# Reordered row loads, weight loads and row normalisation in a two-layer gated cross-attention kernel

## The reference

```python
x = x + tanh(g_xattn[0]) * _L0_xattn_ref(_layernorm(x), ctx_512, Wq, w_kc_q, w_kc_kv, W_qr, W_kr, Wo)
x = x + tanh(g_ffn[0])   * _L0_ffn_ref(_layernorm(x), Wr, br, W1, b1, W2, b2, A1, B1, A2, B2)
x = x + tanh(g_xattn[1]) * _L1_xattn_ref(_layernorm(x), ctx_512, Wq, Wkv_expand, Wout)
x = x + tanh(g_ffn[1])   * _L1_ffn_ref(_layernorm(x), U, V, W1, b1, W2, b2)
...
# _L0_xattn_ref: 16 heads
q_r = einsum('bshq,hqr->bhsr', einsum('bshk,hkq->bshq', q_hk, w_kc_q), W_qr)
scores = einsum('bhsr,bhlr->bhsl', q_r, einsum('bld,hdr->bhlr', kv_rope, W_kr))
attn = softmax(scores)                       # called P in the kernel
ctx_c = einsum('bhsl,bld->bhsd', attn, kv_rope)
out = einsum('bhsd,hkd->bshk', ctx_c, w_kc_kv).reshape(b, s, H * K) @ Wo.T
...
# _L1_ffn_ref: 8 low-rank experts, mixed softly
alpha = softmax(relu(x @ W1 + b1) @ W2 + b2)
vx = einsum('krd,bsd->bskr', V, x)
out = einsum('bsk,bskd->bsd', alpha, einsum('kdr,bskr->bskd', U, vx))
```

## Time and profile before

| | us |
|---|---|
| three runs, median | 1366.28 (1364.13 to 1367.78) |
| profiled execution, its own time | 1366.01 |
| its span | 1364.2 |
| TensorE busy in the span | 1338.5 (98%) |
| VectorE / ScalarE / GpSimd busy | 937.1 / 519.0 / 408.3 |
| DMA, mean over the span | 108 GB/s |

### The profile page before, as it was taken

How to read it: one execution, slowest core, us unless ns; L and a number is a source line. 1 busy time by engine, 2 the same in 40 slices (tenths; PEclk the granted TensorE clock), 3 DMA queues, 4 the chain that set the end, 5 groups by cost and what they waited for, 6 DMA issues and landing times.

```text
span 1364.2 us, 20490 instructions
## 1 busy us (share of the span) xinstructions
PE 1338.5 (98%) x7532; PEld 1083.8 (79%) x7532; DVE 937.1 (69%) x1803; ACT 519.0 (38%) x1569; POOL 408.3 (30%) x463
## 2 busy tenths in 40 slices
PE   7999999999999999999999999999999999999999
PEld 5788888888878788778887888788876788878777
DVE  5666676675775878785778667866888777746533
ACT  2545445455554321231123111311137777712220
POOL 3113313232255343101111111114418865530000
PEclk9999999999999999999999999999999999999999
DMA  8655444443563232210221012112333131144431
GB/s 273 211 164 172 153 157 149 151 157 125 179 208 97 80 94 71 81 39 16 67 89 43 20 43 90 31 58 66 116 110 121 46 103 63 56 142 147 136 124 54
DMA packets 120136, 146.73 MB, mean 108 GB/s; under 512 B 14157, under 2 KB 75725, under 8 KB 120037
## 3 DMA queue, kind: packets, MB, share of 16 engines
q1 hardware_dynamic: 120036, 145.44, 33.5%
HBM read 101.35 MB, written 44.04 MB: 107 GB/s over the span
## 4 chain that ended last, share of the span: by engine, by line
PE 84%; DVE 9%; DMA 2%; SPq 1%; issue 1%; POOL 1%; ACT 1%; DVEq 0%; ACTq 0%; POOLq 0%
PE bank L118 80%; PE bank L121 3%; SPq L170 1%; DVE AH L130 1%; DVE STG L130 1%; DVE st L152 1%; DVE XR L140 1%; DVE PYZ L164 1%; DMA XR<-scr 1%; DVE sm L143 1%; DMA PYZ<-pscr 1%; DVE PT L130 0%; DVE XR L137 0%; DVE AH L127 0%; ACT STG L124 0%
## 5 line engine op out<-in xcount | busy, mean ns | idle before, releaser
L118 PE MATMUL bank<-XT,AR 128*128 128x512 f32 x1152 | 280.2, 393 | 0.1
L118 PE MATMUL bank<-AR 128*128 128x512 f32 x1056 | 260.5, 396 | 1.1 <-DVE PTV L127 0.7
L118 PEld LDWEIGHTS bank<-XT,AR 128*128 128x128 f32 x1152 | 213.9, 188 | 48.5 <-issue 1.5
L124 ACT ACTIVATE STG<-bank,b1c 128x512 f32<-128x512 f32 x128 | 88.3, 690 | 387.2 <-PE bank L118 319.2
L118 PEld LDWEIGHTS bank<-AR 128*128 128x128 f32 x1056 | 193.7, 188 | 46.1 <-DVE AR L130 1.5
L118 PE MATMUL bank<-AR,CT 128*128 128x512 f32 x768 | 191.3, 392 | 0.0
L118 PE MATMUL bank<-AR,AH 128*128 128x512 f32 x768 | 185.8, 390 | 0.0
L127 DVE CAST AH<-STG 128x512 fp32r<-128x512 f32 x192 | 91.3, 475 | 112.8 <-PE bank L118 98.8
L118 PEld LDWEIGHTS bank<-AR,AH 128*128 128x128 f32 x768 | 143.6, 188 | 30.7 <-issue 1.1
L118 PEld LDWEIGHTS bank<-AR,CT 128*128 128x128 f32 x768 | 140.1, 188 | 27.0 <-issue 0.4
L127 POOL CAST BA<-STG 128x256 fp32r<-128x256 f32 x64 | 31.2, 488 | 395.9 <-PE bank L118 251.8
(11 more groups left out here) (142 smaller groups left out, 1858.1 us busy)
## 6 DMA issues: line engine op xcount, KB each, us to landing
XR<-scr SPq DMA_DIRECT2D x64, 256.0 KB, 2.9
pscr<-PYZ SPq DMA_DIRECT2D x30, 512.0 KB, 2.7
PYZ<-pscr SPq DMA_DIRECT2D x120, 128.0 KB, 3.0
XR<-in_x_dram SPq DMA_DIRECT2D x32, 256.0 KB, 4.1
XR<-lscr SPq DMA_DIRECT2D x128, 64.0 KB, 2.0
scr<-XR SPq DMA_DIRECT2D x32, 256.0 KB, 2.1
STG<-in_WoT_dram SPq DMA_DIRECT2D x8, 512.0 KB, 5.3
STG<-in_Wq_dram SPq DMA_DIRECT2D x8, 512.0 KB, 5.9
```

The lines of the kernel that those rows point to most:

```text
L118: return self.e.matmul(o, w, x, start=start, stop=stop, skip_group_check=True) if self.e else Nothing()
L124: return self.e.activation(o, x, func, **kw) if self.e else Nothing()
```

## The change

Four things are moved. No operation is added or taken away.

- **Start**: SP issues the other three blocks of the first group's rows right behind the first block and the identity, ahead of pair 0's `kcqT` and `Wqr`. TensorE transposes two blocks before `prep_a(0)`, not one. VectorE takes all four statistics early, with `ln_turn` and `prep_a` behind.
- **Weights' loads in the first group**: the first block of the second group's rows is requested ahead of the loop, `prep_b(4)` too. `prep_a(5)` and `prep_b(5)` stand ahead of `p_store(1)`, `prep_a(6)` ahead of `p_store(2)`; `ln_store` stands ahead of `p_store` in every unit with p = 3 to 6.
- **Rows between the halves**: in p = 3 to 6 of all four groups VectorE does `ln_norm` and `ln_blocks` before it takes the low part of `pv1`'s second half, and so before `blocks1`.
- **Last stage**: rows of group 2 are loaded between `v_store` and `v_back` of m = 0, rows of group 3 at m = 1 ahead of its first `v_store`.

```diff
--- before.py
+++ after.py
@@ -815,9 +815,10 @@
                         False, True).then_inc(*ps.fill(("acc2", m, tb)))
 
             pe.wait_ge(*d_id[0])
-            ln_turn(0, 0, 0, ring4.next())
+            for tb in range(2):
+                ln_turn(0, 0, tb, ring4.next())
             prep_a(0)
-            for tb in range(1, 4):
+            for tb in range(2, 4):
                 ln_turn(0, 0, tb, ring4.next())
             prep_b(0)
             kv_turn(0)
@@ -1698,13 +1699,14 @@
             ln_norm(0, 0, 0)
             ln_pre(0, 0, 2)
             ln_norm(0, 0, 1)
-            ln_turn(0, 0, 0)
-            prep_a(0)
             ln_pre(0, 0, 3)
             ln_norm(0, 0, 2)
+            ln_turn(0, 0, 0)
             ln_norm(0, 0, 3)
-            for tb in range(1, 4):
-                ln_turn(0, 0, tb)
+            ln_turn(0, 0, 1)
+            prep_a(0)
+            ln_turn(0, 0, 2)
+            ln_turn(0, 0, 3)
             prep_b(0)
             kv_turn(0)
             for u in range(NU + 3):
@@ -1723,13 +1725,13 @@
                     pv1(u - 3, (0,))
                 if u + 1 < 8:
                     prep_b(u + 1)
+                if u < NU and 3 <= p <= 6:
+                    ln_norm(*after1(m), p - 3)
+                    ln_blocks(*after1(m), p - 3)
                 if 3 <= u < NU:
                     pv1(u - 3, (1,))
                 if 1 <= u < 31:
                     blocks1(u - 1)
-                if u < NU and 3 <= p <= 6:
-                    ln_norm(*after1(m), p - 3)
-                    ln_blocks(*after1(m), p - 3)
                 if u < NU and p == 7 and m + 1 < NM:
                     kv_turn(m + 1)
                 if u < NU and 4 <= p <= 7:
@@ -2335,10 +2337,9 @@
 
             ln_load(0, 0, 0)
             e.dma(ident[:, :], i["ident"]).then_inc(*d_id.mark(0))
-            ln_load(0, 0, 1)
+            for tb in range(1, 4):
+                ln_load(0, 0, tb)
             prep_a(0)
-            ln_load(0, 0, 2)
-            ln_load(0, 0, 3)
             e.dma(g4[:, :], i["g4"]).then_inc(*d_g.mark(0))
             kv_load(0)
             e.dma(cs[:, :, :], i["cs"]).then_inc(*d_cs.mark(0))
@@ -2353,12 +2354,14 @@
             prep_a(3)
             prep_b(3)
             prep_a(4)
+            ln_load(*after1(0), 0)
+            prep_b(4)
             for u in range(NU + 3):
                 m, p = divmod(u, 8)
                 if u < NU and 4 <= p <= 7:
                     ln_back(*after1(m), p - 4)
                 if u < NU and 2 <= p <= 4:
-                    for tb in ((0,), (1, 2), (3,))[p - 2]:
+                    for tb in ((0,) if m else (), (1, 2), (3,))[p - 2]:
                         ln_load(*after1(m), tb)
                 if 2 <= u < NU:
                     p_load(u - 2)
@@ -2378,22 +2381,21 @@
                     e.dma(slots[0], i["B2T"]).then_inc(*d_slot[0].mark(("wab", 2)))
                 if u < NU and p == 6 and m + 1 < NM:
                     kv_load(m + 1)
+                if u == 2:
+                    prep_a(5)
+                    prep_b(5)
+                if u == 3:
+                    prep_a(6)
+                if u < NU and 3 <= p <= 6:
+                    ln_store(*after1(m), p - 3)
                 if 1 <= u < 31:
                     p_store(u - 1)
-                if u == 1:
-                    prep_b(4)
-                    prep_a(5)
-                if u == 2:
-                    prep_b(5)
-                    prep_a(6)
                 if u == 3:
                     prep_b(6)
                 if u == 4:
                     prep_a(7)
                 if u == 5:
                     prep_b(7)
-                if u < NU and 3 <= p <= 6:
-                    ln_store(*after1(m), p - 3)
                 if 4 <= u < NU and (u - 4) % 8 == 7:
                     for b in (2, 3):
                         x_store("fin", 0, (u - 4) // 8, b, ("acc", (u - 4) // 8, b))
@@ -2520,9 +2522,6 @@
 
             for m in range(NM):
                 more = m + 1 < NM
-                if m and more:
-                    for tb in range(4):
-                        ln_load(3, m + 1, tb)
                 if m:
                     for tb in range(4):
                         n = 4 * ((m - 1) % 2) + tb
@@ -2532,8 +2531,14 @@
                             e.wait_ge(*stored(3, m + 1, tb))
                             e.dma(X4[:, n, :], rows(3, m + 1, tb)).then_inc(*d_x4[n].mark(m + 1))
                 if more:
+                    if m == 1:
+                        for tb in range(4):
+                            ln_load(3, 3, tb)
                     for tb in range(4):
                         v_store(m, tb)
+                        if m == 0 and tb:
+                            for k in ((0,), (1,), (2, 3))[tb - 1]:
+                                ln_load(3, 2, k)
                         if tb:
                             v_back(m, tb - 1)
                     v_back(m, 3)
```

## The result

The changed kernel takes **1354.86 us**, the median of four runs (1354.11 to 1355.45). The kernel before took 1365.20 beside it (four runs). The ratio is 0.992, with a 95% interval of 0.9903 to 0.9936. A repeat gave 1354.76 against 1365.54, again 0.992 (0.9902 to 0.9938). So the change takes 10.3 to 10.8 us, against the 9.0 forecast. The direction was right and the time lies in the range, near its lower end. But several terms of the sum were wrong, and they cancelled in part. The whole change is 0.8% of the time, so its single terms are read from the traces more than from medians.

The account below looks back on a forecast made before the run. TensorE was taken to bound the kernel, with only its idle time (25.7 us) or lower-clock time to win back. The terms 1.6 + 3.1 + 2.0 + 2.3 = 9.0 us off 1366.0 gave 1357.0 us, range 1354.4 to 1361.1.

Parts of the forecast that it names:

- Part 1: Start: reordered row loads, transposes and statistics remove waits for blocks 2 and 3; 1.6 us, bounds 0 to 2.8.
- Part 3: Rows' normalisation and transpose moved into VectorE's idle time, so TensorE's waits for maxima go; 2.0 us, bounds 0.8 to 2.1.
- Part 2: Unit 3: earlier row block and moved weights' loads shorten the value product's wait; 3.1 us, bounds 0 to 3.4.
- All it can give back is time in which TensorE stands still or runs at the lower clock: Whole kernel: no work leaves TensorE, so gains come only from 25.7 us idle in 1364.2 or lower-clock time.
- I assume that it moves with G: Start: the clock's rise, behind 19.5 us, shifts with G; if it stays, 0.8 of 1.6 us is lost.
- The clock follows: Unit 3: after the 1.81 us idle the clock falls to 1.2 GHz; avoiding that gives 0.67 + 0.93 = 1.6 us.
- after the other 13 units of this form TensorE does not wait, and they give nothing: Rows between the halves: only three listed waits, together 2.1 us, can give anything; 13 other units give none.
- Part 4: Last stage: row blocks requested 13 us earlier, so TensorE's wait for the normalised block goes; 2.3 us, bounds 2.0 to 2.3.
- The start gives nothing: Rival at the start: clock rises late, or block 1 and M's weights land late; 1358.6 us, chance 0.16.
- unit 3 keeps a wait: Rival in unit 3: P's low part is late by another road and the clock falls; 1360.1 us, chance 0.09.
- part 3's collision: Rival: moved normalisation collides with GpSimd, gain 0.8 or none; 1358.2 to 1359.0 us, chance 0.08.
- slower: Rival: the moved pair delays P's transposes and road through DRAM in 16 units; 1378 us, chance 0.03.

Follow-up runs that it names:

- a1_order: Kernel before with only TensorE's and VectorE's new orders at the start, SP's load queue as it was; 1364.15 us against 1366.36, ratio 0.9987.
- warm_after: Changed kernel plus 14 unused identity transposes while TensorE would wait for the first rows; 1354.63 us against the kernel before's 1365.54, ratio 0.9913.
- a_start: Kernel before with only the start's changes (row loads first, two blocks transposed early, statistics early); 1362.41 us against 1365.23, ratio 0.9979.
- b1_row_early: Kernel before with only the first row block of group 1 requested one unit earlier, weights' loads unmoved; 1364.63 us against 1366.36, ratio 0.9989.
- b_weights: Kernel before with only the first group's row block and weights' loads moved around P's transfers; 1363.42 us against 1365.23, ratio 0.9983.
- c_halves: Kernel before with only normalisation and block transpose ahead of CT's second half, and rows' store ahead of P's; 1362.51 us against 1365.23, ratio 0.9978.
- warm_before: Kernel before plus 14 unused identity transposes in TensorE's idle time ahead of its first transpose; 1366.22 us against 1366.36, ratio 1.0001.
- fill_both: Changed kernel plus 14 identity transposes at the start and 8 in stage 3's 1.43 us wait; 1354.14 us, ratio 0.9916 against the kernel before.
- no_start: Changed kernel with the start's changes undone, the other three parts kept; 1356.42 us, ratio 0.9929 against the kernel before.

## Why the prediction was right or wrong

The steps of the prediction that failed are terms of its sum. Part 1 has the clock's rise only move along with G, 1.6 us for 3.78 in the profile. Part 3 says of the other 13 units that they give nothing, and prices a wait at its listed 0.93, 2.0 for 3.71. Part 2 takes the clock's fall as certain (1.6 of its 3.1 us), and stage 3's loss of 1.57 was put at nothing. The waits and the order of events behind the parts were right. That the time came near is in part luck: the errors have both signs.

**What bounds the kernel: right, with a gap.** Every wait that was named went, and TensorE's idle time fell to 18.2 where 18.5 was forecast. But of the 11.1 us only 7.5 are idle time. Of the 3.6 less busy time, the clock explains 1.9 (start 1.88 gained, unit 3 about 1.6 gained, stage 3 1.57 lost). The other 1.7 are small stalls that the records count as busy (below, at part 3). "All it can give back is time in which TensorE stands still or runs at the lower clock" was right only if the idle time is not read off the list of waits.

**Part 1: too low, 1.6 for 3.78 in the profile.** The order gave 1.90, as reckoned: the gap before block 1 was 0.28 where 0.5 was put, and M was covered. Of the 0.3 for rows that land sooner 0.1 came (VectorE's idle before block 1's statistics is 1.42, for 1.53). The step that failed is "I assume that it moves with G". G moved by 1.9, and the rise of the clock by more than 5: in the kernel before G ran slow to its end at 19.5, in the changed one it ran fast from 14.02. The profiles with the old order (without added work) have G at 2.8 to 3.6 us, each with waits of about 1.0 and 0.8 ahead. The kernels with the whole of part 1 and no added work have it at 1.94 to 2.59. `a1_order` decides between an earlier G and fewer pauses: G at the same time as before, no pause behind 10.90, and 1.92 us long. So closing the two waits moved the clock's rise too. From the lengths of G and of the product behind it I estimate the rise at 17.8 to 20.2 us in the six kernels with the old start, and at 14.2 to 15.2 in the three with the new one. It is no certainty in a single execution: `warm_after` has G at 2.88 without a pause of note ahead. I had the rows for this, and priced the waits as lost time alone. The Trainium skill, in "TensorE: Matmul & The Clock Gate", section "What you observe", has the rise come after sustained activity, varying by half a microsecond from run to run. The direction agrees: what is no longer interrupted rises sooner. The size of the variation is larger here. G among kernels with one and the same start is 1.94, 2.15 and 2.59 long, which by my estimate puts the rises up to 1.3 us apart, counted from the first transpose. I had used this section for the small variation and not for the interruptions.

On average over profiles the first scores come 2.9 us sooner (28.0 in the three profiles with part 1 and no added work, 30.9 in the six without). Part of the 3.78 was luck, the profile of before being the latest of its six and that of the changed kernel the earliest of its three. In runs without a fall part 1 is worth 2.1 (`a_start`) and 2.3 (in company).

**Part 2: the size right, one of its two halves by chance.** The wait went from 1.81 to 0.50 (0.2 was forecast). `b1_row_early` shows that both causes that were named counted: the row block took the unit from 16.3 to 16.8 us (without a fall) to 15.71, P's way back the other 1.0. The step that failed is "The clock follows", 1.6 us taken as certain. Of seven profiles with a wait of 1.78 or more there, the clock fell in two (the kernel before, and `a1_order`). One profile of the kernel before could not show that. With no fall to remove, part 2 is worth some 1.8 us by the lengths of unit 3, and `b_weights` alone measured 1.8 between medians. Between runs without a fall it is only 0.8 (1362.65 for 1363.46, 5 and 18 runs), and nothing here explains the difference.

**Part 3: too low, 2.0 for 3.71.** The mechanism was right, without a price to pay: in `c_halves` too the maxima come early enough and no TensorE wait for `sm` is left. The collision with GpSimd that was feared does occur, clearly once in the 16 units (a normalisation took 1.30 at 386.55 in the changed kernel, 0.66 in one other and 0.54 in the rest), and costs TensorE no wait. The sum was under-counted twice. First, a wait of 0.93 costs more than 0.93. The products of scores at both ends of unit 30, in the kernel before and in the changed one:

```profile
387.78 1.16 PE L118 MATMUL bank<-K,Q 64*128 64x128 f32 x16
...
400.58 1.16 PE L118 MATMUL bank<-K,Q 64*128 64x128 f32 x16
```

```profile
378.40 1.16 PE L118 MATMUL bank<-K,Q 64*128 64x128 f32 x16
...
390.10 1.16 PE L118 MATMUL bank<-K,Q 64*128 64x128 f32 x16
```

That is 12.80 and 11.70 here, and 12.81 and 11.64 in the unit before: 1.1 and 1.2 for a listed 0.93. The rows show where the rest lies. Without a wait the value product starts ahead of the recorded end of the product before it (384.39, for 383.03 + 1.52 = 384.55), and the idle time is counted from that end: 0.16 more. After a wait it also takes 0.95 and not 0.88. Second, "after the other 13 units of this form TensorE does not wait, and they give nothing" was false for three of them. Units 12, 20 and 28 were 11.96 long and are 11.64 now, with no idle time listed in either kernel (most units of this stage are 11.64 long, not the 13 put down ahead of the prediction):

```profile
175.25 1.16 PE L118 MATMUL bank<-K,Q 64*128 64x128 f32 x16
...
187.21 1.16 PE L118 MATMUL bank<-K,Q 64*128 64x128 f32 x16
```

```profile
167.99 1.16 PE L118 MATMUL bank<-K,Q 64*128 64x128 f32 x16
...
179.63 1.16 PE L118 MATMUL bank<-K,Q 64*128 64x128 f32 x16
```

In unit 12 the same value product started 0.09 behind the recorded end of the one before it, too little for the list, and 0.25 later than it can. 2.27 + 3 x 0.32 + 0.49 (the wait of 0.3 after unit 6) = 3.7. A look at the lengths of the units before the prediction would have shown all of it: equal units, unequal lengths.

**Part 4: right**, 2.25 for 2.3 in the profile. Over the other kernels that wait varies from 1.36 to 1.94 (and 2.73 in `warm_before`), so 1.9 is the fairer size (the mean of seven, 1.7, and 0.2 for the wait a turn before). The cover that was named held: the transfers behind the four row loads came later, and TensorE did not wait.

**What was not in the prediction: stage 3.** Its waits of 0.67 and 1.43 are the same in all kernels. The clock fell behind them in three of thirteen profiles (`fill_both`, where the wait was filled, not counted): the changed kernel twice, and `c_halves`. All three contain part 3, but so do `no_start` and `warm_after`, in which it did not fall, so part 3 does not bring it for certain. None of the eight profiles without part 3 had it. Three of thirteen drawn at random would all lie among these five in 10 of 286 cases. That part 3 causes it is not shown either, since nothing that it moves lies near stage 3. It stays open. In six runs `no_start` had no fall and the changed kernel had one in five of ten, which leaves open as well whether part 1 has a share. (`c_halves`, without part 1, reads below 1.000 in 11 of 12, but that counts falls in unit 3 too.)

**The rivals.** None came true. "The start gives nothing" is refuted by 2.9, "unit 3 keeps a wait" by 0.50 without a fall, part 3's collision by 3.71, and "slower" by the even 11.64 of the units. The sum with the terms corrected, and no fall on either side, is 2.9 + 1.8 + 3.7 + 1.9 = 10.3, where runs without a fall show 9.3. These are medians of 18 and 5 runs, and the first scores alone vary by 1.4 us between profiles with the same start (30.05 to 31.42), so the 1.0 between the two is not explained further.

## What to carry to other kernels

In a kernel of many equal units, list the start of each unit's first product and compare the lengths before you list waits: a stall of 0.3 us showed in no list of waits, and 0.93 on the row was 1.2 in time. Price a gap in TensorE's work twice where the clock is low or may fall: closing two waits at the start brought the fast clock some 3 to 6 us forward, but a fall seen in one profile is one draw, to be entered with a chance and not as a certainty. An order and the loads that feed it are one change: at the start the new order alone gave 1.6 us from the first transpose to the first scores, the new loads alone nothing, and both together about 3.4.

## What the runs showed of the hardware

- After waits of 1.78 to 1.95 us in unit 3, with the same work around them, TensorE's clock fell in two of seven profiles. In the kernel before it then stayed at 1.2 GHz for 3.4 us and cost 0.9 to 1.4 us of the unit's length against the four profiles with the wait, no fall and no added work (16.26 to 16.83). Behind 0.67 and 1.43 us in stage 3 it fell in three of thirteen. Behind 2.73 us in the last stage it fell once more (`warm_before`, a clock of 0.83 from 1290 to 1300), and behind 1.36 to 2.08 in the same place in none of seven.
- Three of four runs of the kernel before had at least one fall, and much of the spread between runs comes with it: 1363.5 without, 1366.5 with.
- The clock, once up, can be lost at the start too: 14 added transposes raised it to 2.4 GHz by 7.95 us, and behind waits of 0.67 and 1.81 it was at 1.2 GHz again (`warm_before`). The same transposes ahead of the changed order raised it by M in one of two profiles (M 1.45 and 2.66 us).
- With G at the same place (15.92 and 15.96) its four passes took 3.62 us behind pauses of 0.99 and 0.80, and 1.92 us where no pause stood behind 10.90 (`a1_order`).
- TensorE's busy time fell by 3.6 us with the number and shapes of its instructions the same.
